# A body of half width for an expert's last rows, one packed table value an expert, and unrolled programs on ScalarE and VectorE

## The chip, the cores and the metric

The kernel runs on one core of a Trainium2 chip. What is compared is the device time of one launch in microseconds: 1143.42 us, the median of three timed runs (1143.06 to 1143.54). The core has TensorE (matmuls), VectorE, ScalarE and GpSimd, and SyncE, which issues most of the DMAs. Each of them runs its own program, and they meet only in semaphores.

## The reference

One transformer layer for 8 sequences of 512 rows and 256 columns: cross-attention with 16 heads over a context of 1024 rows, then a mixture of experts. The feed-forward half is what matters here:

```python
ys = _geglu(xf @ Ws1 + bs1) @ Ws2 + bs2
logits = (xf @ Wr + br) / TAU
top_val, top_idx = jax.lax.top_k(logits, 2)
top_w = jax.nn.softmax(top_val, axis=-1)
...
h = jnp.einsum('nd,edh->enh', xf, We1) + be1[:, None, :]
act = _geglu(h)
yE = jnp.einsum('enh,ehd->end', act, We2) + be2[:, None, :]
yr = jnp.einsum('end,ne->nd', yE, w)
return (ys + yr).reshape(B, T, Dm)
```

There are 4096 rows and 12 experts, and every row goes to two of them, so the experts work on 8192 rows in all. An expert's hidden layer is 2 x 768 wide; `_geglu` multiplies one half of it by the gelu of the other. A kernel need not compute an expert for rows that didn't choose it: this one sorts.

## The kernel before

Attention writes each row, normalised, into a region of `expert_in` in DRAM for each of its two experts, one region an expert. In `feed_forward` VectorE's `tables()` works out how many blocks of `NB` = 256 rows each expert has (`blocks_i`) and the number of its first block (`first_i`), and for each block where in `expert_in` it starts. The shared feed-forward `ys` is done in blocks of the same size; after it the expert stage runs from about 605 us to the end.

*The order of the work.* Nothing is scheduled by a planner: each engine runs the same nest of loops, written by `experts(eng, before, body, piece)` at line 1954. It loops over pairs of experts (`half`, line 1991; the sixth pair is written out behind the loop), so that the buffers of even and odd experts have fixed addresses. At the start of a pair `both` reads four table values into registers. `one` then walks an expert's blocks: on every engine a turn for block `t` is run only if `t < n`, so an expert of three blocks has one empty turn of the four (`FEW`); a copy of the body for blocks from the fifth on lies behind it and is jumped over by experts of at most four. ScalarE and VectorE have one more copy ahead, of two turns (`lead`), in which they also split the next expert's weights into a high and a low half in 16 bits, twelve pieces, one beside each of the six pairs of a block. If an expert has fewer than two blocks, the pieces of the missing ones are done alone.

*A block.* Its rows come from `expert_in` to `ff_xrow` (`load_rows` on SyncE, line 2051; the row's weights and target follow in `ff_rowmeta`). TensorE transposes them (line 2156) during the block before; ScalarE and VectorE make the high half `xh` and the low half `xl`. In `ffn` (line 2160) TensorE then makes the hidden layer in six pairs `j`: 2 halves x 2 tiles x 3 products = 12 matmuls of 128x128 weights on 256 columns. For each pair ScalarE takes the gelu (`ff_gel`, line 2236), VectorE multiplies (`ff_actf`, 2373), ScalarE makes the high half (`ff_acth`, 2231), VectorE the low one (`ff_actl`, 2366). TensorE may be three pairs ahead (three banks). Then it transposes the next block's rows, and the output layer follows: for each pair, for each of the two tiles of 128 rows, 3 matmuls (line 2182). VectorE adds the bias (`ff_ysb`, 2437; one addition for each tile), ScalarE scales by the row's weight (`ff_ysc`, 2282), and GpSimd adds the rows to the output with two indirect DMAs (line 2140). `ff_ysc` is a single buffer: the scaling of a block waits until the DMAs of the block before have landed (`row_done`). So is `ff_rowmeta`: SyncE loads the next one when GpSimd has taken the targets (`t_set`), and issues the rows of the block after that behind it.

*Between experts* GpSimd waits for the split of the expert's weights, sets `ff_taken` and issues the load of the weights of the expert after next (2.3 MB); ScalarE and VectorE copy the expert's biases (`biases_ready`, lines 2270 and 2441); TensorE waits for the split weights (line 2211).

Of the kernel before, what the change touches and what calls it, by code (L numbers as in the profile page):

```python
# [10 lines left out]
P = 128  # L11
# [1801 lines left out]
FEW = 4  # L1813
SH_PAIRS, EX_PAIRS = HS // P, HR // P
# [33 lines left out]
SEEN = 4  # L1848
LISTS = [(0, 0), (0, 1), (1, 0), (1, 1), (1, 2), (1, 3)]
# [4 lines left out]
def feed_forward(nc, io, keep, scratch, shared, expert, early):  # L1854
# [17 lines left out]
    first_i = sb("first_i", [P, E + 1], I32)  # L1872
# [33 lines left out]
    b1a = sb("b1a", [P, EX_PAIRS], FP32)  # L1906
    b1g = sb("b1g", [P, EX_PAIRS], FP32)
# [17 lines left out]
    e_now = sb("e_now", [P, 1], FP32)  # L1925
# [16 lines left out]
    b2_loaded, e_set, g_set, a_set = (semaphore(n) for n in ("b2_loaded", "e_set", "g_set", "a_set"))  # L1942
# [11 lines left out]
    def experts(eng, before, body, piece=None):  # L1954
# [3 lines left out]
        def one(half, u, n, at, last):  # L1958
            e = half * 2 + u
            if before:  # L1960
                before(e, u, last)

            def own(t, beside=None):
                with eng.If(t < n):
                    body(e, u, nc.s_assert_within(at + t, 0, NBLK - 1, skip_runtime_bounds_check_because=
                                               "t < n, and an expert's last block is within all experts' blocks"), beside)

            lead = 0
            if piece and (not last or u == 0):
# [8 lines left out]
            with eng.Fori(lead, FEW) as t:  # L1978
                own(t)
            with eng.If(n > FEW):  # L1980
                with eng.Fori(1, N // NB // FEW) as group:
                    with eng.If(n > group * FEW):
                        with eng.Fori(0, FEW) as t:
                            own(group * FEW + t)

        def both(half, last):
            sizes = [table(eng, blocks_i, half * 2 + u, N // NB) for u in range(2)]
            firsts = [table(eng, first_i, half * 2 + u, NBLK - 1) for u in range(2)]
            for u in range(2):
                one(half, u, sizes[u], firsts[u], last)  # L1990
# [12 lines left out]
    def _(sp):  # L2003
# [60 lines left out]
        experts(sp, None, lambda e, u, n, beside: load_rows(n + 1))  # L2064
        until(expert, "meta_loaded", of(expert, "meta_loaded", table(sp, first_i, E, NBLK), 16))
# [426 lines left out]
```

## Time and profile before

| | |
|---|---|
| median of the timed runs | 1143.42 us |
| the profiled execution | 1138.47 us |
| its span, first to last instruction | 1136.9 us |
| TensorE busy over the span | 994.1 us (87%) |
| VectorE, ScalarE, GpSimd busy | 722.5, 578.4, 369.9 us |
| mean granted clock of TensorE | 0.969 |
| expert stage | 605 us to the end |

Busy time of TensorE counts pipelined matmuls, whose ends are modelled; how long a group takes from start to start is told by the chain of waits better. "Issue" is time in which an engine waited for nothing that the profile shows: it is where its sequencer reads tables, branches, or has no code yet. A row's line is that of the kernel's source, and the lines 1952 to 1991 are those of the loops around a block.

### The profile page before, as it was taken

What the parts mean: (1) busy time and instruction counts of PE and PEld (TensorE: products, weight loads), DVE (VectorE), ACT (ScalarE), POOL (GpSimd) and SP (SyncE); (2) the same over time, 40 slices, a digit from 0 to 9 for tenths busy, and PEclk for the clock granted to TensorE, in tenths of its full rate; (3) what the DMA queues carried; (4) which work ended last, traced back from release to release, by engine and by line L of the source; (5) the groups of instructions that cost most, each with busy time, mean ns of one, the idle gap of its engine ahead of it and who ended that gap; (6) DMA issues with size and microseconds to landing.
All of it is one profiled execution on the core that took longest, in us unless ns stands there. A gap on an engine that the chain in (4) does not pass through costs nothing.

```text
span 1136.9 us, 26307 instructions
## 1 busy us (share of the span) xinstructions
PE 994.1 (87%) x7659; PEld 729.5 (64%) x7660; DVE 722.5 (64%) x1862; ACT 578.4 (51%) x1289; POOL 369.9 (33%) x536
## 2 busy tenths in 40 slices
PE   5678889888998879788998998979998999898995
PEld 3233434444443438676777887869887888787884
DVE  5766777777787645455775765657565666565653
ACT  2135555555555664233534655646454664555652
POOL 5200121435426352073001433334233343333332
PEclk9789999999999999989999999989999999999998
DMA  5524414334532222168434434244233452424232
GB/s 154 140 69 104 99 62 123 96 104 132 126 94 76 99 79 69 40 236 273 149 110 133 103 66 119 42 123 121 44 91 77 116 128 40 123 44 116 48 49 29
DMA packets 105808, 114.98 MB, mean 101 GB/s; under 512 B 20092, under 2 KB 97864, under 8 KB 105552
## 3 DMA queue, kind: packets, MB, share of 16 engines
q1 hardware_dynamic: 85072, 66.08, 21.2%
q0 software_dynamic: 20064, 47.20, 16.8%
q8 instruction: 31, 0.51, 0.2%
q14 instruction: 81, 0.66, 0.2%
q10 hardware_dynamic: 560, 0.53, 0.1%
HBM read 73.64 MB, written 37.25 MB: 98 GB/s over the span
## 4 chain that ended last, share of the span: by engine, by line
PE 38%; issue 8%; DMA 5%; DVE 2%; ACT 1%; POOL 1%; SPq 1%; ACTq 1%; POOLq 0%; DVEq 0%
PE ff_psH L2171 23%; PE ff_psY L2182 14%; DMA ff_xrow<-expert_in 2%; DMA out_dram<-ff_ysc,ff_trow 2%; PE ff_psX L2156 2%; DMA ff_xrow<-xn 1%; DVE ff_actf L2373 1%; DVE ff_actl L2366 1%; DVE ff_ysb L2437 0%; ACTq L1952 0%; DMA out_dram<-ff_x 0%; SPq L1952 0%; ACT ff_ysc L2282 0%; POOL out_dram L2140 0%; ACT ff_wx L2257 0%
## 5 line engine op out<-in xcount | busy, mean ns | idle before, releaser
L2171 PE MATMUL ff_psH<-xh,ff_wx 128*128 128x256 f16 x1872 | 321.1, 276 | 27.3 <-issue 23.0
L2171 PE MATMUL ff_psH<-xl,ff_wx 128*128 128x256 f16 x936 | 258.4, 276 | 0.0
L1122 DVE TENSOR_REDUCE fast_negm<-fast_psS 128x2 f32<-128x512 f32 x256 | 169.2, 686 | 86.6 <-PE fast_psS L513 85.0
L2171 PEld LDWEIGHTS ff_psH<-xh,ff_wx 128*128 128x128 f16 x1872 | 185.4, 99 | 55.9 <-issue 25.8
L884 ACT ACTIVATE fast_PT<-fast_psT 128x512 f32<-128x512 f32 x256 | 145.7, 598 | 71.4 <-PE fast_psT L545 71.1
L2140 POOL DMA_INDIRECT out_dram<-ff_ysc,ff_trow x78 | 123.5, 1583 | 168.2 <-ACT ff_ysc L2282 142.6
L2373 DVE SCALAR_TENSOR_TENSOR ff_actf<-ff_psH,ff_b1a,ff_gel 128x256 f32<-128x256 f32 x234 | 112.5, 481 | 89.4 <-ACT ff_gel L2236 89.3
L2182 PE MATMUL ff_psY<-ff_wx,ff_acth 128*128 128x256 f16 x936 | 155.4, 273 | 0.0
L2236 ACT ACTIVATE ff_gel<-ff_psH,ff_b1g 128x256 f32<-128x256 f32 x234 | 109.5, 468 | 60.4 <-PE ff_psH L2171 49.8
L2231 ACT ACTIVATE ff_acth<-ff_actf 128x256 f16<-128x256 f32 x282 | 115.6, 410 | 29.1 <-DVE ff_actf L2373 27.0
L2182 PE MATMUL ff_psY<-ff_wx,ff_actl 128*128 128x256 f16 x468 | 127.6, 273 | 0.0
L513 PE MATMUL fast_psS<-fast_Kz,fast_Qs 128*128 128x512 f16 x256 | 98.3, 396 | 29.6 <-DVE fast_negm L1122 21.7
L2366 DVE TENSOR_TENSOR ff_actl<-ff_actf,ff_acth 128x256 f16<-128x256 f32 x282 | 117.6, 417 | 4.0 <-ACT ff_acth L2231 1.9
L545 PE MATMUL fast_psT<-fast_Qs,fast_Kz 128*128 128x512 f16 x256 | 96.7, 383 | 12.6 <-ACT fast_PT L884 12.2
L2171 PEld LDWEIGHTS ff_psH<-xl,ff_wx 128*128 128x128 f16 x936 | 92.8, 99 | 11.4
L2182 PEld LDWEIGHTS ff_psY<-ff_wx,ff_acth 128*128 128x128 f16 x936 | 91.6, 98 | 10.1
L2282 ACT ACTIVATE ff_ysc<-ff_ysb,ff_wrow 128x256 f32<-128x256 f32 x78 | 35.4, 500 | 113.8 <-DVE ff_ysb L2437 113.8
L2395 DVE TENSOR_TENSOR ff_wx<-ff_st,ff_wx x144 | 79.9, 555 | 15.7 <-ACT ff_wx L2257 11.5
L1456 POOL TENSOR_SCALAR fast_rstd<-fast_mv 128x4 f32<-128x4 f32 x16 | 3.6, 227 | 221.1 <-DVE fast_mv L1074 196.1
L2257 ACT ACTIVATE ff_wx<-ff_st x144 | 73.8, 512 | 1.6 <-issue 1.3
L545 PEld LDWEIGHTS fast_psT<-fast_Qs,fast_Kz 128*128 128x128 f16 x256 | 24.8, 99 | 75.0 <-ACT fast_PT L884 41.7
L561 PE MATMUL fast_psV<-fast_PT,fast_V 128*32 128x512 f32 x512 | 69.1, 612 | 3.1 <-ACT fast_PT L884 1.7
(260 smaller groups left out, 1621.3 us busy)
## 6 DMA issues: line engine op xcount, KB each, us to landing
ff_st<-in_L_ffn_We_dram POOLq DMA_DIRECT2D x12, 1536.0 KB, 7.3
ff_xrow<-expert_in SPq DMA_DIRECT2D x40, 256.0 KB
ff_st<-in_L_ffn_We_dram POOLq DMA_DIRECT2D x12, 768.0 KB, 8.9
fast_Qs<-qstk SPq DMA_DIRECT2D x48, 128.0 KB
fast_xbuf<-in_x_dram SPq DMA_DIRECT2D x8, 512.0 KB, 4.9
fast_words<-in_mask_BxSxS_bk_dram SPq DMA_DIRECT2D x8, 512.0 KB, 3.8
fast_xres<-in_x_dram SPq DMA_DIRECT2D x8, 512.0 KB, 4.0
out_dram<-fast_x1s SPq DMA_DIRECT2D x8, 512.0 KB, 5.0
```

What stands on the lines that cost most here:

```text
L513: mm = nc.tensor.matmul(out[:], qs(b)[:, p, t * P:(t + 1) * P], kz(b, c)[:, p, :, :], start=True, stop=not general)
L545: mm = nc.tensor.matmul(out[:], kz(b, kb // 2)[:, h // 2, h % 2, (kb % 2) * P:(kb % 2 + 1) * P], qs(b)[:, h // 2, :], start=True, stop=not ...
L884: nc.scalar.activation(PT[:, n % NPT, :], psT[n % 2][:], ACT.Exp).then_inc(sem["exp_done"], 1)
L1122: nc.vector.tensor_reduce(negm[:, two(b), t, 2 * p:2 * p + 2], src, AX.X, ALU.max, negate=True).then_inc(sem["max_done"], 1)
L2140: pool.indirect_dma_start(out=out_rows, out_offset=bass.IndirectOffsetOnAxis(ap=trow[:, j:j + 1], axis=0), in_=ysc[:, j, :], in_offset=Non ...
L2171: mm = nc.tensor.matmul(psH[j % stage.banks][:, half * NB:(half + 1) * NB], a[:, dt, lo:lo + P], x[:, dt, :], start=(dt == 0 and i == 0), ...
L2182: mm = nc.tensor.matmul(psY[i][:, 0:D], a[:, j, i * P:(i + 1) * P], x[:, j, :], start=(j == 0 and s == 0), stop=(j == n - 1 and s == 2))
L2231: nc.scalar.activation(acth[:, j, :], actf[:, j % 2, :], ACT.Copy).then_inc(stage.sem["acth"], 1)
L2236: nc.scalar.activation(gel[:, j % 2, :], psH[j % stage.banks][:, NB:2 * NB], ACT.Gelu, bias=gate_bias[:, j:j + 1]).then_inc(stage.sem["gel ...
L2366: nc.vector.tensor_tensor(actl[:, j, :], actf[:, j % 2, :], acth[:, j, :], ALU.subtract)\
L2373: nc.vector.scalar_tensor_tensor(actf[:, j % 2, :], psH[j % stage.banks][:, 0:NB], bias[:, j:j + 1], gel[:, j % 2, :], ALU.add, ALU.mult). ...
L2395: nc.vector.tensor_tensor(wx[u][1][:, cols], st[u][:, cols], wx[u][0][:, cols], ALU.subtract).then_inc(w_low, 1)
```

## The change

What was a block of 256 rows always becomes 256 rows as long as an expert has as many, and its rest, if it is 1 to 128 rows, goes through a body of half width: 128 columns in each hidden matmul, one tile of output rows instead of two, and 128 elements in the four operations of ScalarE and VectorE on a pair. A rest of 129 to 256 rows takes the full body as before. Loading, transposing, scaling and adding to the output stay at 256 rows; the unused half of `ff_ysb` is set to zero once. The number of units of 128 rows and the first block of an expert are packed in one table value (`place_i`), which is taken apart in registers, so that an engine reads one value for an expert instead of two.

TensorE, GpSimd and SyncE keep the loop over pairs of experts; GpSimd and SyncE have no half body. TensorE's single loop of four turns becomes two of two turns, with a test around the second, the copy for the fifth block on is inside that test, and the half body stands behind it. ScalarE and VectorE are written out for the twelve experts, each reading its one value at its start; their copies of the biases go, as the addresses are now fixed.

```diff
-    def experts(eng, before, body, piece=None):
+    def place_of(eng, e):
+        value = nc.values_load(place_i[0:1, bass.ds(e, 1)], engines=[eng.engine], min_val=0, max_val=NBLK * PLACE + PLACE - 1,
+                               skip_runtime_bounds_check_because="built on chip from counts whose sum is two rows a token")
+        return value & (PLACE - 1), value >> PLACE.bit_length() - 1
+
+    def experts(eng, before, body, piece=None, halves=True, unrolled=False):
 
         eng.wait_ge(table_ready, 1)
 
-        def one(half, u, n, at, last):
-            e = half * 2 + u
+        def one(e, u, units, at, last):
             if before:
                 before(e, u, last)
+            n = (units >> 1) if halves else (units + 1) >> 1
+
+            def block_at(t):
+                return nc.s_assert_within(at + t, 0, NBLK - 1, skip_runtime_bounds_check_because=
+                                          "t < n, and an expert's last block is within all experts' blocks")
 
             def own(t, beside=None):
                 with eng.If(t < n):
-                    body(e, u, nc.s_assert_within(at + t, 0, NBLK - 1, skip_runtime_bounds_check_because=
-                                               "t < n, and an expert's last block is within all experts' blocks"), beside)
+                    body(e, u, block_at(t), beside, NB)
 
             lead = 0
-            if piece and (not last or u == 0):
+            if piece and not last:
                 lead = PIECES // EX_PAIRS
                 with eng.Fori(0, lead) as t:
                     def beside(j):
-                        piece(e + 1, half + (1 + u), 1 - u, at, t * EX_PAIRS + j, j == 0)
+                        piece(e + 1, (e + 1) // 2 + 1, 1 - u, at, t * EX_PAIRS + j, j == 0)
                     own(t, beside)
                     with eng.If(t >= n):
                         for j in range(EX_PAIRS):
                             beside(j)
-            with eng.Fori(lead, FEW) as t:
-                own(t)
-            with eng.If(n > FEW):
-                with eng.Fori(1, N // NB // FEW) as group:
-                    with eng.If(n > group * FEW):
-                        with eng.Fori(0, FEW) as t:
-                            own(group * FEW + t)
+            if lead < FEW // 2:
+                with eng.Fori(lead, FEW // 2) as t:
+                    own(t)
+            with eng.If(n > FEW // 2):
+                with eng.Fori(FEW // 2, FEW) as t:
+                    own(t)
+                with eng.If(n > FEW):
+                    with eng.Fori(1, N // NB // FEW) as group:
+                        with eng.If(n > group * FEW):
+                            with eng.Fori(0, FEW) as t:
+                                own(group * FEW + t)
+            if halves:
+                with eng.If((units & 1) > 0):
+                    body(e, u, block_at(n), None, UN)
+
+        if unrolled:
+            for e in range(E):
+                one(e, e % 2, *place_of(eng, e), e == E - 1)
+            return
 
         def both(half, last):
-            sizes = [table(eng, blocks_i, half * 2 + u, N // NB) for u in range(2)]
-            firsts = [table(eng, first_i, half * 2 + u, NBLK - 1) for u in range(2)]
+            places = [place_of(eng, half * 2 + u) for u in range(2)]
             for u in range(2):
-                one(half, u, sizes[u], firsts[u], last)
+                one(half * 2 + u, u, *places[u], last)
         with eng.Fori(0, E // 2 - 1) as half:
             both(half, False)
         both(E // 2 - 1, True)
...
-        def ffn(stage, m, wa, wb, more):
+        def ffn(stage, m, wa, wb, more, rows=NB):
...
-                            mm = nc.tensor.matmul(psH[j % stage.banks][:, half * NB:(half + 1) * NB], a[:, dt, lo:lo + P],
-                                                  x[:, dt, :], start=(dt == 0 and i == 0), stop=(dt == DT - 1 and i == 2))
+                            mm = nc.tensor.matmul(psH[j % stage.banks][:, half * NB:half * NB + rows], a[:, dt, lo:lo + P],
+                                                  x[:, dt, 0:rows], start=(dt == 0 and i == 0), stop=(dt == DT - 1 and i == 2))
...
-                for i in range(NBT):
+                for i in range(rows // P):
...
-                nc.scalar.activation(gel[:, j % 2, :], psH[j % stage.banks][:, NB:2 * NB], ACT.Gelu,
+                nc.scalar.activation(gel[:, j % 2, 0:rows], psH[j % stage.banks][:, NB:NB + rows], ACT.Gelu,
...
-        def biases_ready(e, u, last):
-            nc.scalar.activation(b1g[:], b1T[:, bass.ds((e * 2 + 1) * EX_PAIRS, EX_PAIRS)], ACT.Copy).then_inc(g_set, 1)
-            act.wait_ge(g_set, e + 1)
-            if not isinstance(e, int):
-                act.sem_inc(alone, 1)
...
-        experts(act, biases_ready, expert_rows, high_piece)
+        experts(act, None, expert_rows, high_piece, unrolled=True)
...
+            then(nc.vector.scalar_tensor_tensor(first[:], first[:], float(PLACE), units[:], ALU.mult, ALU.add))
+            nc.vector.tensor_copy(place_i[:], first[:])
...
-        experts(dve, biases_ready, expert_block, low_piece)
+        experts(dve, None, expert_block, low_piece, unrolled=True)
```

TensorE, the end of an expert's first copy of the body. Before, `L1978` ends the loop of four turns and `L1980` jumps over the copy for blocks from the fifth on, one copy of 245 instructions (a weight load, which has no row of its own here, counted with each matmul):

```order
L2182 MATMUL ff_psY<-ff_wx,ff_acth 128x256 x2
L2182 MATMUL ff_psY<-ff_wx,ff_actl 128x256
L1964 UNCONDITIONAL_BRANCH
L1978 REGISTER_ALU
L1978 COMPARE_AND_BRANCH
L1980 COMPARE_AND_BRANCH
L1981 UNCONDITIONAL_BRANCH
```

Now `L1989` ends a loop of two turns and `L1991` jumps over two copies, 491 instructions:

```order
L2204 MATMUL ff_psY<-ff_wx,ff_acth 128x256 x2
L2204 MATMUL ff_psY<-ff_wx,ff_actl 128x256
L1975 UNCONDITIONAL_BRANCH
L1989 REGISTER_ALU
L1989 COMPARE_AND_BRANCH
L1991 REGISTER_ALU x2
L1991 COMPARE_AND_BRANCH
L1992 UNCONDITIONAL_BRANCH
L1975 COMPARE_AND_BRANCH
```

Its target is the test for the half body, whose hidden matmuls have 128 columns:

```order
L2000 REGISTER_ALU
L2000 COMPARE_AND_BRANCH
L79 ISA x2
L2193 MATMUL ff_psH<-xh,ff_wx 128x128
L2193 MATMUL ff_psH<-xl,ff_wx 128x128
L2193 MATMUL ff_psH<-xh,ff_wx 128x128 x2
```

With two such parts the loop over pairs, from the table loads to its branch back, grows from 996 instructions to 1880.

ScalarE, from the end of one expert to the first gelu of the next. Before, at the end of a pair (`L1991` branches back to the first load of the loop; these loads are those of the last pair, which look the same):

```order
L1991 REGISTER_ALU
L1991 COMPARE_AND_BRANCH
L1952 TENSOR_LOAD ff_blocks_i
L1952 ISA x2
L1952 TENSOR_LOAD ff_blocks_i
L1952 ISA x2
L1952 TENSOR_LOAD ff_first_i
L1952 ISA x2
L1952 TENSOR_LOAD ff_first_i
L1952 ISA x2
L2271 ACTIVATE ff_b1g<-ff_b1T 128x6
L1971 UNCONDITIONAL_BRANCH
```

Now, between two experts that are written out one behind the other:

```order
L2298 ACTIVATE ff_ysc<-ff_ysb,ff_wrow 128x256 x2
L2000 UNCONDITIONAL_BRANCH
L1957 TENSOR_LOAD ff_place_i
L1981 UNCONDITIONAL_BRANCH
L1975 REGISTER_ALU x2
L1975 COMPARE_AND_BRANCH
L79 ISA
L79 REGISTER_ALU
L2258 ACTIVATE ff_gel<-ff_psH,ff_b1T 128x256
```

Three loads of four, the copy of the biases and the branch back are gone, and the stored program is longer: an expert has about 160 instructions on ScalarE and 190 on VectorE, times twelve.

## Rows read from the trace of the kernel before

**Rows 1.** Busy time by stretch: expert stage, and start of expert 4.

```profile
core 0: us, PE busy (x) PEld busy (x) DVE busy (x) ACT busy (x) POOL busy (x), PEclk, DMA share, GB/s
608.62:1124.30 515.68, 487.74 (x4368) 430.45 (x4368) 314.50 (x817) 293.62 (x726) 181.04 (x264) 0.98 0.38 87
757.00:762.00 5.00, 3.28 (x16) 2.35 (x17) 0.33 (x2) 0.00 (x0) 2.52 (x2) 0.50 0.63 104
```

**Rows 2.** Chain of waits: start us, us, what; one full block.

```profile
661.16 7.86 PE ff_psH L2171 x72
669.02 0.44 PE ff_psX L2156 x4
669.45 3.93 PE ff_psY L2182 x36
```

**Rows 3.** Page, part 5: the output DMAs, two a block.

```profile
L2140 POOL DMA_INDIRECT out_dram<-ff_ysc,ff_trow x78 | 123.5, 1583 | 168.2 <-ACT ff_ysc L2282 142.6
```

**Rows 4.** VectorE's timeline: start us, us; additions of a block's result.

```profile
673.54 0.76 DVE L2437 TENSOR_TENSOR ff_ysb<-ff_psY,ff_b 128x256 f32<-128x256 f32 x2 [1.83 <-PE ff_psY L2182]
685.76 0.76 DVE L2437 TENSOR_TENSOR ff_ysb<-ff_psY,ff_b 128x256 f32<-128x256 f32 x2 [1.83 <-PE ff_psY L2182]
...
703.63 0.76 DVE L2437 TENSOR_TENSOR ff_ysb<-ff_psY,ff_b 128x256 f32<-128x256 f32 x2 [0.65 <-PE ff_psY L2182]
...
753.71 0.76 DVE L2437 TENSOR_TENSOR ff_ysb<-ff_psY,ff_b 128x256 f32<-128x256 f32 x2 [0.63 <-PE ff_psY L2182]
...
773.11 0.76 DVE L2437 TENSOR_TENSOR ff_ysb<-ff_psY,ff_b 128x256 f32<-128x256 f32 x2 [0.92 <-PE ff_psY L2182]
...
917.17 0.84 DVE L2437 TENSOR_TENSOR ff_ysb<-ff_psY,ff_b 128x256 f32<-128x256 f32 x2 [1.84 <-PE ff_psY L2182]
...
929.58 0.76 DVE L2437 TENSOR_TENSOR ff_ysb<-ff_psY,ff_b 128x256 f32<-128x256 f32 x2 [0.66 <-PE ff_psY L2182]
...
942.82 0.76 DVE L2437 TENSOR_TENSOR ff_ysb<-ff_psY,ff_b 128x256 f32<-128x256 f32 x2 [0.60 <-PE ff_psY L2182]
...
967.29 0.76 DVE L2437 TENSOR_TENSOR ff_ysb<-ff_psY,ff_b 128x256 f32<-128x256 f32 x2 [1.83 <-PE ff_psY L2182]
...
985.63 0.76 DVE L2437 TENSOR_TENSOR ff_ysb<-ff_psY,ff_b 128x256 f32<-128x256 f32 x2 [0.65 <-PE ff_psY L2182]
```

**Rows 5.** Chain of waits at the branches back before experts 2 and 4.

```profile
687.26 3.02 issue
...
690.37 0.28 ACTq L1952
...
691.01 0.27 ACTq L1952
...
753.55 5.17 issue
758.72 9.86 PE ff_psH L2171 x72
```

**Rows 6.** Table loads: ns min/median/max, first and last start.

```profile
L1952 ACTq TENSOR_LOAD <-ff_blocks_i x12: 272/283/381, 603.6 to 1050.9; - x12
L1952 PEldq TENSOR_LOAD <-ff_blocks_i x12: 296/307/323, 604.5 to 1048.3; - x12
```

**Rows 7.** TensorE's branches: over unexecuted code, and back (ns min/median/max).

```profile
L2002 PEldq COMPARE_BRANCH  x1: 3485/3485/3485, 481.1 to 481.1; - x1
...
L1991 PEldq COMPARE_BRANCH  x5: 76/208/219, 684.3 to 1047.5; - x5
```

**Rows 8.** DMA queues, 700 to 1040 us: packets, MB, share; q8 has none.

```profile
q0 software_dynamic: 11040, 25.43, 31.5%
q1 hardware_dynamic: 14144, 7.03, 8.6%
q14 instruction: 33, 0.27, 0.3%
```

**Rows 9.** TensorE's timeline: matmuls of one column, each with its load.

```profile
594.99 1.94 PE L2206 MATMUL ff_psB<-ones,ff_wx 128*128 128x1 f16 x72
```

**Rows 10.** Groups by line, expert stage: busy us, mean ns; idle before.

```profile
L2171 PEld LDWEIGHTS ff_psH<-xh,ff_wx 128*128 128x128 f16 x1872 | 185.4, 99 | 55.9 <-issue 25.8 <-DVE ff_actf L2373 6.5
...
L2373 DVE SCALAR_TENSOR_TENSOR ff_actf<-ff_psH,ff_b1a,ff_gel 128x256 f32<-128x256 f32 x234 | 112.5, 481 | 89.4 <-ACT ff_gel L2236 89.3
L2236 ACT ACTIVATE ff_gel<-ff_psH,ff_b1g 128x256 f32<-128x256 f32 x234 | 109.5, 468 | 60.4 <-PE ff_psH L2171 49.8 <-ACT ff_b1g L2271 4.1
L2366 DVE TENSOR_TENSOR ff_actl<-ff_actf,ff_acth 128x256 f16<-128x256 f32 x238 | 99.2, 417 | 3.0 <-ACT ff_acth L2231 1.5
L2231 ACT ACTIVATE ff_acth<-ff_actf 128x256 f16<-128x256 f32 x238 | 97.5, 410 | 21.2 <-DVE ff_actf L2373 19.2
...
L2395 DVE TENSOR_TENSOR ff_wx<-ff_st,ff_wx x132 | 73.2, 554 | 13.9 <-ACT ff_wx L2257 11.5 <-issue 2.3
L2257 ACT ACTIVATE ff_wx<-ff_st x132 | 67.6, 512 | 1.6 <-issue 1.3
...
L2222 ACT ACTIVATE xh<-ff_psX 128x512 f16<-128x512 f32 x40 | 23.1, 578 | 0.0
```

**Rows 11.** VectorE's timeline: the last low half ahead of expert 4.

```profile
752.06 0.42 DVE L2366 TENSOR_TENSOR ff_actl<-ff_actf,ff_acth 128x256 f16<-128x256 f32 x1
```

**Rows 12.** Landing of a scatter in the chain; TensorE's waits for rows.

```profile
639.50 3.74 DMA out_dram<-ff_ysc,ff_trow
...
PE ff_psX L2156 <- DMA ff_xrow<-expert_in: 4.0, 5, 1.3
```

More of the change, by code:

```diff
@@ L1813 @@
 FEW = 4
+UN = P
 SH_PAIRS, EX_PAIRS = HS // P, HR // P
@@ L1848 @@
 SEEN = 4
+PLACE = 64
 LISTS = [(0, 0), (0, 1), (1, 0), (1, 1), (1, 2), (1, 3)]
@@ L2063, in _ @@
         store_out(NSH - 1)
-        experts(sp, None, lambda e, u, n, beside: load_rows(n + 1))
-        until(expert, "meta_loaded", of(expert, "meta_loaded", table(sp, first_i, E, NBLK), 16))
+        experts(sp, None, lambda e, u, n, beside, rows: load_rows(n + 1), halves=False)
+        until(expert, "meta_loaded", of(expert, "meta_loaded", table(sp, total_i, 0, NBLK), 16))
         until(shared, "saved", of(shared, "saved", NSH))
@@ L2125, in start_expert, with add_rows @@
                 load_weights(e + 2, u)
-        def add_rows(e, u, n, beside):
+        def add_rows(e, u, n, beside, rows):
             expert.until(pool, "meta_loaded", of(expert, "meta_loaded", n, 16), alone=True)
@@ L2144, in add_rows @@
             pool.sem_inc(expert.sem["row_done"], 1)
-        experts(pool, start_expert, add_rows)
+        experts(pool, start_expert, add_rows, halves=False)
     @block.tensor
@@ L2214, in weights_ready @@
                 pe.sem_inc(alone, 1)
-        experts(pe, weights_ready, lambda e, u, n, beside: ffn(expert, n, w1[u], w2[u], (expert, n + 1)))
+        experts(pe, weights_ready, lambda e, u, n, beside, rows: ffn(expert, n, w1[u], w2[u], (expert, n + 1), rows))
     @block.scalar
@@ L2222, in row_high, with ffn @@
             nc.scalar.activation(xh[:].rearrange("p t n -> p (t n)"), psX[:], ACT.Copy).then_inc(stage.sem["xh"], 1)
-        def ffn(stage, m, gate_bias, more, beside=None):
+        def ffn(stage, m, gate_bias, more, beside=None, rows=NB):
             n = stage.pairs
@@ L2230, in high @@
                     stage.until(act, "y_mm", of(stage, "y_mm", m))
-                nc.scalar.activation(acth[:, j, :], actf[:, j % 2, :], ACT.Copy).then_inc(stage.sem["acth"], 1)
+                nc.scalar.activation(acth[:, j, 0:rows], actf[:, j % 2, 0:rows], ACT.Copy).then_inc(stage.sem["acth"], 1)
             for j in range(n):
@@ L2304, in tables @@
             then(nc.vector.tensor_scalar(counts_i[:], counts[:], float(NB - 1), None, ALU.add))
+            nc.vector.tensor_scalar(units[:], counts[:], float(UN - 1), None, ALU.add)
             then(nc.vector.tensor_scalar(blocks_i[:], counts_i[:], NB.bit_length() - 1, None, ALU.logical_shift_right))
+            then(nc.vector.tensor_copy(units_i[:], units[:]))
+            then(nc.vector.tensor_scalar(units_i[:], units_i[:], UN.bit_length() - 1, None, ALU.logical_shift_right))
+            nc.vector.tensor_copy(units[:], units_i[:])
             dve.wait_ge(cleared, 1)
@@ L2357, in row_low, with ffn @@
                                     ALU.subtract).then_inc(stage.sem["xl"], 1)
-        def ffn(stage, m, bias, more, result, beside=None):
+        def ffn(stage, m, bias, more, result, beside=None, rows=NB):
             n = stage.pairs
```

50 lines of the change are left out of this document (22 added, 28 removed).

## The prediction

> **What bounds the kernel now.** I read the page first, for TensorE's share, then the stretches around the expert stage, then the chain of waits of that stage, then VectorE's timeline at the experts' borders, last the code that the borders run and the instruction DMAs.
>
> From 608.6 to 1124.3 us the kernel does nothing but expert blocks, and TensorE is busy for 487.7 of 515.7 us [rows 1]. In the chain a full block of 256 rows is TensorE alone: 7.86 us for the 72 matmuls of the hidden layer, 0.44 us for the next block's transposes, 3.93 us for the 36 of the output layer, together 12.23 us [rows 2]. The output DMAs are 78, two a block, so 39 blocks ran [rows 3], and 39 x 12.23 = 477.0 us; the other 38.7 us lie at the borders of experts. The distance between two result additions on VectorE shows where: 12.22 us inside an expert, 17.87 (685.76 to 703.63), 19.40 and 18.34 us where the loop over pairs of experts jumps back, and 12.41 plus 13.24 us where expert 7 follows 6 [rows 4]. The four jumps back (before experts 2, 4, 6, 8) lose 5.6, 7.2, 6.2 and 6.1 us over 12.23, 25.1 in all, though after each of them every engine reads its tables again. On ScalarE 3.02 us of nothing stand right behind the loop's branch, and only then come the four table loads [rows 5]; a load takes 0.28 us on ScalarE and 0.31 on TensorE [rows 6], on ScalarE about 0.6 from one to the next [rows 5], so on TensorE, whose register work is no shorter, some 0.75. TensorE's own branch back costs 0.21 us and never more than 0.22, but its branch over unexecuted code at 481 us took 3.49 us [rows 7]. Between 700 and 1040 us instruction queue q8, which moved 31 packets of 16 KB over the span (page, part 3) and which I take for TensorE's, moved nothing, though the loop ran round several times [rows 8]. So TensorE's loop (996 instructions, a weight load counted for each matmul) stays in its memory, and those of ScalarE and VectorE (293 and some 340) do not.
>
> **The change, part by part.** From the reference's inputs the experts get 371, 831, 614, 487, 1296, 738, 520, 802, 720, 621, 676, 516 rows. In blocks of 256 that is 39, as the trace has it; in units of 128 it is 70: 31 full bodies and 8 half ones (experts 0, 1, 2, 4, 6, 7, 9, 11).
>
> *Half bodies.* 72 hidden matmuls keep their weight loads and have 128 columns for 256; 36 output matmuls become 18 of unchanged shape; the transposes stay. No 128-column matmul in 16 bits is in the trace. From below: half of 0.109 us is 0.055; from above, if the weight load set the pace, 0.109. 72 loads with one column each took 1.94 us [rows 9], 0.025 us apart, so loads don't set it: 72 x 0.056 = 4.0, + 0.44 + 18 x 0.109 = 2.0, is 6.4 us. ScalarE and VectorE must keep up with 0.67 us a pair: at 256 columns an activation and a copy take 0.47 + 0.41, the two VectorE operations 0.48 + 0.42 [rows 10]. Copies of 256, 384 and 512 columns take 0.41, 0.51, 0.58, so 128 columns save about 0.1 each and a pair needs some 0.65 to 0.7. That leaves the last pair's chain of four small operations sticking out; I take 6.8 us, between 6.4 and 7.8. Eight times 12.23 - 6.8 = 5.4 is **-43.4 us** (-35 to -47).
>
> The Trainium skill speaks against small matmuls: "TensorE: Matmul & The Clock Gate" (Wait — 56ns, not 53.3ns?) gives about 62 ns of sequencer time for each matmul when hardware decode is off. The 0.025 us spacing [rows 9] shows that this doesn't hold here; by it a half body would take some 0.4 us more.
>
> *Expert 0* has one full block. ScalarE and VectorE do the second six pieces of weight splitting with no matmul beside them, before the half body: 6 x 0.51 and 6 x 0.55 us [rows 10] that were hidden. With TensorE's first skip (below) **+4.8**.
>
> *The loop back.* ScalarE and VectorE run straight on: their 3 us gap, three of four loads and two small copies go, so they are ready about 3 us after a block's end and TensorE decides. Its sequencer is 1.1 us ahead of its matmuls: the last low half ends at 752.48, the matmuls at 753.55, and the next ones start at 758.72 [rows 5, 11]. These 6.3 us hold four loads (3.0) and, after an expert of two blocks, two empty loop turns of two 0.21 us branches with their register work each (1.45). After the change two loads remain and the empty iterations are skipped: 3.3 us. I take it as lost: 3.3 us more (3.49 less 0.21 [rows 7]), and the idle time costs 2 us at 1.2 GHz: after the wait of 5.17 us the granted clock was 0.50 [rows 1] and the same 72 matmuls took 9.86 us [rows 5]. Behind a half body the sequencer is only 0.3 us ahead. The four borders then lose 8.6, 7.5, 6.5 and 8.6 = 31.2 for 25.1: **+6.1** (between -14 and +12).
>
> The rule behind this is in "Runtime: NRT & Kernel Launch" (Instruction fetch mechanics): 128 KiB for TensorE, filled in blocks of 16 KiB, and a taken branch out of the window waits for a fetch. By it 1880 instructions of 64 bytes, 117.5 KiB, with a block fetched ahead don't fit; the trace agrees in size with its 3.49 us branch, and has no run of this size.
>
> *Skips.* An expert of one or two full blocks now jumps over two unused copies, 491 instructions or 1.9 pieces; before it was one, 0.95 piece, and cost nothing. The new jump lands beyond the next piece. I count it where the code is reached for the first time: expert 0 (above) and 11, **+3.6** (3.5 + 1.2 of branches - 1.1 ahead). In the loop's later passes the piece may still be there.
>
> *Borders without a jump back.* Before experts 1, 3, 5, 7 TensorE now starts 1 us late (short lead behind a half body). The chain scatter, its landing (3.74 us), target rows, metadata, next rows had 20.1 us from a block's end and already made TensorE wait up to 1.3 us [rows 3, 12]. A half body brings the scatter 1.5 us closer to the one before it. Together about 2.6 us a border where 1.9 were lost: **+3.6**, and **+0.4** before expert 10, which has no branch back but also the short lead.
>
> *The rest.* First start two loads less, -1.3; at the end the last scatter waits for its predecessor, +1. The table's five added VectorE operations and GpSimd's memset lie beside shared blocks, where TensorE is busy; uncovered they would be 1.5 us.
>
> Sum: -43.4 + 4.8 + 6.1 + 3.6 + 3.6 + 0.4 - 0.3 = -25.2. The profiled execution took 1138.5 us, so 1113.3; the median of the timed runs is 4.95 above it, so **1118 us**.
>
> **The rivals.** *A, TensorE's code stays.* For it: q8's silence; against: the loop nearly doubles. The four borders lose 10 to 12 us for 25.1 (-13 for +6.1), expert 11 nothing: -47.9, **1095 us**.
>
> *B, the forecast*: lost at each jump back, kept otherwise.
>
> *C, all its code is fetched anew in each pass*, as the other engines' is now (33 pieces on their queue between 700 and 1040 us [rows 8]). Then the skip also costs at experts 2, 6 and 9 (3.6 each, less 2.8 that hide the row waits), expert 3 stops for its skips twice more and expert 5 once (3.3 each): +18, **1136 us**, within noise of no gain from below.
>
> *D, the weight load sets the pace of narrow matmuls.* Page part 5 has a load at 99 ns and matmuls 109 ns apart [rows 10]. At 0.109 each, a half body's hidden layer stays at 7.86 and loses 72 x 0.054 = 3.9 us, eight times 31: **1149 us**, slower. It turns the result from 0.1 us a matmul on. Against it stands the 0.025 us spacing.
>
> *E, the change doesn't do what it says*: other row counts, fewer halves. 39 blocks fit the counts; 0.01.
>
> **How the numbers follow.** B 0.40, A 0.22, C 0.27, D 0.05, the rest 0.06. B's own range, by the half body and the borders, is 1108 to 1128. The 8-in-10 range takes in A and most of C: 1092 to 1142. A measurement tells 0.2%, 2.3 us, from no change. A and B are faster, C is in two thirds of its spread, D is slower: faster 0.80, same 0.09, slower 0.11.
>
> **What would show it.** Half bodies: result additions 6.4 to 7.8 us apart, 128-column matmuls 0.056 us apart; at 0.109 it is D. ScalarE's and VectorE's "issue" waits at borders under 3 us. TensorE: branch rows of the loop back at about 3.5 us and q8 active between experts 2 and 9 for B and C, silent for A; 3.5 us at experts 2, 3, 6, 9 for C. Wrong I would be if half bodies took over 8 us, or if TensorE waited at a border for rows for more than 3 us.

## The result and the profile after

The changed kernel took 1148.58 us (median of 8 runs, 1145.5 to 1153.11), the kernel before 1143.24 us on the same chip. The ratio is 1.006, with a 95% interval of 1.0038 to 1.0082: about 6 us slower. Forecast were 1118 us. Of the kernels below, dead_code alone had runs more than 1.5% slower than its fastest; these two of its four are left out of its ratio.

First the page of the profiled execution (1145.5 us, span 1143.6): busy time by engine, the instruction queue that I had taken for TensorE's, and the costliest group with its idle time (31 packets, and 23.0 us for want of instructions, in the kernel before).

```profile
PE 967.9 (85%) x7515; PEld 704.6 (62%) x7516; DVE 709.5 (62%) x1834; ACT 568.7 (50%) x1276; POOL 366.2 (32%) x537
...
q8 instruction: 73, 1.20, 0.4%
...
L2193 PE MATMUL ff_psH<-xh,ff_wx 128*128 128x256 f16 (+1 forms) x1872 | 302.6, 273 | 62.2 <-issue 60.1
```

The windows of the expert stage, of the wait before expert 4 and of the block behind it. They answer to [rows 1]: stretch, length, busy time by engine, granted clock, DMA share, GB/s.

```profile
608.74:1130.90 522.16, 455.90 (x4224) 404.20 (x4224) 300.63 (x786) 284.06 (x715) 175.81 (x260) 0.94 0.38 87
760.60:770.60 10.00, 10.00 (x74) 8.25 (x75) 5.25 (x13) 5.65 (x14) 2.65 (x7) 0.79 0.58 222
755.00:761.00 6.00, 0.40 (x3) 0.29 (x4) 0.00 (x0) 0.00 (x0) 1.55 (x1) 0.50 0.56 93
```

The stage takes 522.2 us for 515.7, though TensorE is busy for 31.8 us less: it is idle for 66.3 us where it was for 27.9, and its granted clock fell from 0.98 to 0.94.

The chain of waits (start us, us, what) shows a half body, and what stands before expert 4, which answers to the 5.17 us of [rows 5].

```profile
746.89 3.93 PE ff_psY L2204 x36
750.82 9.78 issue
760.60 10.02 PE ff_psH L2193 x72
...
912.45 4.19 PE ff_psH L2193 x72
...
917.08 1.98 PE ff_psY L2204 x18
```

The body itself is what was forecast: with 0.44 us of transposes between the two rows it takes about 6.6 us, and 6.4 where nothing disturbs it; its 128-column matmuls start 0.056 us apart. Behind the full block before it, though, TensorE waits 2.66 us for want of instructions. The wait before expert 4 has nearly doubled. VectorE's additions say the same, against [rows 4]:

```profile
750.85 0.76 DVE L2458 TENSOR_TENSOR ff_ysb<-ff_psY,ff_b 128x256 f32<-128x256 f32 x2 [0.64 <-PE ff_psY L2204]
775.02 0.75 DVE L2458 TENSOR_TENSOR ff_ysb<-ff_psY,ff_b 128x256 f32<-128x256 f32 x2 [1.16 <-PE ff_psY L2204]
...
909.83 0.76 DVE L2458 TENSOR_TENSOR ff_ysb<-ff_psY,ff_b 128x256 f32<-128x256 f32 x2 [1.31 <-PE ff_psY L2204]
919.09 0.42 DVE L2458 TENSOR_TENSOR ff_ysb<-ff_psY,ff_b 128x256 f32<-128x256 f32 x1
```

24.17 us over the border before expert 4 (19.40 before the change); 9.3 us for expert 6's half body with the skip ahead of it. All eight half bodies are 8.6 to 14.0 us from the addition before, though the prediction had 6.4 to 7.8 and named over 8 us as a sign of being wrong. Over the four borders with a jump back the distances are 20.05, 24.17, 23.92 and 19.88 us: 39.1 us over 12.23, for 25.1.

TensorE's branches, ns min/median/max, first and last start (in [rows 7] the branch back never took over 219). L1991 jumps over two copies of the body (the one for the third and fourth block and the one for blocks from the fifth on), L2000 over the half body, L2012 is the branch back.

```profile
L1991 PEldq COMPARE_BRANCH  x12: 67/198/4496, 620.7 to 1120.5; - x12
L2000 PEldq COMPARE_BRANCH  x12: 68/77/3388, 625.4 to 1124.1; - x12
L2012 PEldq COMPARE_BRANCH  x5: 67/3604/4593, 681.7 to 1055.4; - x5
```

From 600 us on, 13 of these branches take 2.1 to 4.6 us, 45.6 us in all: four at the branch back, four at L2000 (behind experts 3, 5, 8 and 10, which have no half body), five at L1991 (experts 0, 2, 6, 9 and 11). Three of them, at expert 0, behind expert 10 and at expert 11, are at code that is reached for the first time: experts 10 and 11 are the sixth pair, written out behind the loop. Behind expert 3 two come in a row, 3.14 us at 750.58 and 4.59 us at 753.88; these are the 9.78 us of the chain. Between 700 and 1040 us, where q8 was silent [rows 8], it moves 31 packets:

```profile
q8 instruction: 31, 0.51, 0.6%
```

### The profile page after: what moved, and what is told of

Its sections match the earlier page's. It is cut to its first block, busy times and chain, and to the rows that moved or that the text cites. A ratio compares the mean times of both kernels' runs of the same rounds, so it can differ in the third digit from the quotient of the medians.

```text
span 1143.6 us, 25763 instructions
## 1 busy us (share of the span) xinstructions
PE 967.9 (85%) x7515; PEld 704.6 (62%) x7516; DVE 709.5 (62%) x1834; ACT 568.7 (50%) x1276; POOL 366.2 (32%) x537
## 4 chain that ended last, share of the span: by engine, by line
PE 39%; issue 10%; DMA 4%; DVE 2%; SPq 1%; ACT 1%; POOL 1%; POOLq 0%; DVEq 0%; ACTq 0%
PE ff_psH L2193 25%; PE ff_psY L2204 13%; PE ff_psX L2178 2%; DMA ff_xrow<-expert_in 2%; DMA out_dram<-ff_ysc,ff_trow 1%; DMA ff_xrow<-xn 1%; DVE ff_actl L2387 1%; DVE ff_actf L2394 0%; POOL out_dram L2162 0%; SPq L1954 0%; ACT ff_ysc L2298 0%; DMA out_dram<-ff_x 0%; ACT ff_gel L2258 0%; PE ff_psB L2228 0%; DVE ff_ysb L2458 0%
## 5 line engine op out<-in xcount | busy, mean ns | idle before, releaser
L2193 PE MATMUL ff_psH<-xh,ff_wx 128*128 128x256 f16 (+1 forms) x1872 | 302.6, 273 | 62.2 <-issue 60.1
L2193 PE MATMUL ff_psH<-xl,ff_wx 128*128 128x256 f16 (+1 forms) x936 | 249.2, 273 | 0.0
L2394 DVE SCALAR_TENSOR_TENSOR ff_actf<-ff_psH,ff_b1T,ff_gel 128x256 f32<-128x256 f32 (+1 forms) x234 | 106.2, 454 | 153.1 <-ACT ff_gel L2258 151.8
L2258 ACT ACTIVATE ff_gel<-ff_psH,ff_b1T 128x256 f32<-128x256 f32 (+1 forms) x234 | 105.8, 452 | 122.3 <-PE ff_psH L2193 109.2
L2204 PE MATMUL ff_psY<-ff_wx,ff_acth 128*128 128x256 f16 x840 | 140.5, 274 | 0.0
L2253 ACT ACTIVATE ff_acth<-ff_actf 128x256 f16<-128x256 f32 (+1 forms) x282 | 110.1, 390 | 22.6 <-DVE ff_actf L2394 21.2
L2204 PE MATMUL ff_psY<-ff_wx,ff_actl 128*128 128x256 f16 x420 | 114.8, 273 | 0.0
L2387 DVE TENSOR_TENSOR ff_actl<-ff_actf,ff_acth 128x256 f16<-128x256 f32 (+1 forms) x282 | 111.0, 393 | 4.1 <-ACT ff_acth L2253 3.0
L2193 PEld LDWEIGHTS ff_psH<-xl,ff_wx 128*128 128x128 f16 x936 | 96.5, 103 | 10.0
L2204 PEld LDWEIGHTS ff_psY<-ff_wx,ff_acth 128*128 128x128 f16 x840 | 82.5, 98 | 9.5
L545 PEld LDWEIGHTS fast_psT<-fast_Qs,fast_Kz 128*128 128x128 f16 x256 | 25.1, 100 | 76.9 <-ACT fast_PT L884 40.0
```

Source lines behind the costliest of these rows:

```text
L545: mm = nc.tensor.matmul(out[:], kz(b, kb // 2)[:, h // 2, h % 2, (kb % 2) * P:(kb % 2 + 1) * P], qs(b)[:, h // 2, :], start=True, stop=not ...
L2193: mm = nc.tensor.matmul(psH[j % stage.banks][:, half * NB:half * NB + rows], a[:, dt, lo:lo + P], x[:, dt, 0:rows], start=(dt == 0 and i = ...
L2204: mm = nc.tensor.matmul(psY[i][:, 0:D], a[:, j, i * P:(i + 1) * P], x[:, j, :], start=(j == 0 and s == 0), stop=(j == n - 1 and s == 2))
L2253: nc.scalar.activation(acth[:, j, 0:rows], actf[:, j % 2, 0:rows], ACT.Copy).then_inc(stage.sem["acth"], 1)
L2258: nc.scalar.activation(gel[:, j % 2, 0:rows], psH[j % stage.banks][:, NB:NB + rows], ACT.Gelu, bias=gate_bias[:, j:j + 1]).then_inc(stage. ...
L2387: nc.vector.tensor_tensor(actl[:, j, 0:rows], actf[:, j % 2, 0:rows], acth[:, j, 0:rows], ALU.subtract)\
```

## The experiments

**Theory 1:** TensorE's pair loop, grown from 996 to 1880 instructions (1878 in the texts and pads below), no longer stays in the engine's memory, and its code is fetched anew in each pass. **Theory 2:** the long jump over two unused copies costs it, whatever the loop's size. **Theory 3:** something else of the change is at fault (unrolled programs of ScalarE and VectorE, half bodies). The first four kernels ran on one chip (kernel before: 1142.57 us), the seven others on a second one (1179.24 and 1180.39 us). There the expert stage begins some 34 us later and takes the same time: the kernel short_loop, traced on both, has its first hidden matmul of an expert at 609.4 and 643.3 us, and from there to its last matmul 487.0 and 484.7 us. So between the chips only ratios are compared.

**short_loop.** The changed kernel, but TensorE has one loop of four turns for an expert's full bodies: 1396 instructions.

```
-            if lead < FEW // 2:
-                with eng.Fori(lead, FEW // 2) as t: own(t)
-            with eng.If(n > FEW // 2):
-                with eng.Fori(FEW // 2, FEW) as t: own(t)
+            with eng.Fori(0, FEW) as t: own(t)      # TensorE alone
```

> The changed kernel with one edit on TensorE alone: one loop of four turns over an expert's blocks, as before, instead of two of two turns, so one full copy less for each expert and a loop over pairs of 1396 instructions instead of 1878. Theory 1 (TensorE's loop no longer stays in its memory, and its branches wait for code): all branches of 2 to 4.6 us vanish, q8 moves nothing in the middle of the expert stage, and most of their 47 us come back: 1095 to 1108 us. Theory 2 (the half bodies and the earlier work of the other engines bring waits of their own, for rows or for GpSimd, and the branches only hide them): 1135 to 1150 us.

Measured: 1112.33 us, ratio 0.973 (0.9711 to 0.9749). Of 13 long branches two are left, both where code is reached for the first time; q8 and the branch back:

```profile
q8 instruction: 34, 0.56, 0.2%
...
L2020 PEldq COMPARE_BRANCH  x5: 76/207/212, 680.9 to 1018.8; - x5
```

This one loop turns 1.006 into 0.973, some 38 us, more than the whole error of the forecast, though unrolled programs and half bodies are still in it. Theory 3 falls as the cause of the loss. Theory 1's 1095 to 1108 us is missed by 4 us all the same: with its code in place the kernel has other waits, below.

**dead_code.** The kernel before with 219 matmuls for each expert behind conditions that are never true; TensorE's loop has 1878 instructions.

```
+                if unused:
+                    with eng.If(n > N // NB - 1): unused(121)
+            if unused:
+                with eng.If(n > N // NB - 1): unused(98)
```

> The kernel before, with matmuls that are never executed placed where the changed kernel has its extra copies on TensorE (121 after the copy for blocks from the fifth on, 98 more behind it, for each expert; the loop over pairs is 1878 instructions long, as in the changed kernel). Nothing else changes, what is executed is the same. Theory 1: long branches at the same places as in the changed kernel, some 10 of 3 to 4.6 us, and 1170 to 1190 us. Theory 2: code that isn't executed costs two tests an expert, 1143 to 1148 us.

Measured: 1198.64 and 1214.71 us, ratio 1.0558 (1.0475 to 1.0641); the trace is of an execution of 1227.0 us. From 600 us on 24 of its branches take 1.9 us or more, 87.1 us together: twelve at the added skip of 98 matmuls, one for each expert, nine at the skip over the copy and the other 121, three at the branch back. q8 moves 72 packets. Code that is never executed costs 6%, more than the 1170 to 1190 us expected, and half of the long branches stand at a jump that the changed kernel doesn't have. So this run doesn't tell size from jumps.

**unrolled_only** and **halves_only.** Both have short_loop's TensorE loop. The first has no half bodies (the rest of an expert takes a full one), the second keeps ScalarE's and VectorE's rolled loop with its three small copies an expert. Both have the packed table value; no run has it alone.

```
-            n = (units >> 1) if halves else (units + 1) >> 1
+            n = (units + 1) >> 1                    # unrolled_only; no body for UN rows
```

```
-        experts(act, None, expert_rows, high_piece, unrolled=True)
+        experts(act, biases_ready, expert_rows, high_piece)     # halves_only; VectorE likewise
```

> Short TensorE loop, packed table value, ScalarE and VectorE unrolled, but no half bodies. Theory 1: their gaps of 3 us behind the branch back and three loads of four go, TensorE decides at the borders, the four borders with a branch back lose 8 to 13 us instead of 25: 1128 to 1135 us. Theory 2 (the longer programs of ScalarE and VectorE wait for code themselves, or GpSimd's chain takes over): 1140 us or more.

> Short TensorE loop, packed table value, half bodies, but ScalarE and VectorE in the loop over pairs as before. Theory 1: eight half bodies of 6.4 us instead of 12.23 save 47 us, less 3 at expert 0 and 1 to 1.5 at each border behind a half body; the branch back of ScalarE and VectorE stays: 1103 to 1113 us. Theory 2: above 1125 us.

Measured: 1126.01 us, ratio 0.986 (0.9834 to 0.9886), and 1114.18 us, ratio 0.9758 (0.9736 to 0.978). Both lie just outside what was expected, 2 us below and 1 us above. Each part gains without the other, 17 and 28 us (the packed value counted in both), but together 30, not 45. Beside unrolling, half bodies give 14 us, though they take 46.6 us of work away; beside half bodies, unrolling gives 1.9 us, less than the runs of each kernel spread. TensorE's waits in the expert stage (in total, times, longest us), of unrolled_only and then of short_loop, say where the rest goes:

```profile
PE ff_psH L2198 <- issue: 17.6, 12, 3.9
```

```profile
PE ff_psH L2201 <- issue: 29.0, 14, 3.9
PE ff_psX L2186 <- DMA ff_xrow<-expert_in: 10.8, 6, 2.3
PE ff_psH L2201 <- DVE ff_actf L2402: 2.2, 2, 1.7
PE ff_psH L2201 <- DVE xl L2385: 2.0, 5, 1.2
```

26.4 us of waits come back. 10.8 of them are waits for rows, which unrolled_only doesn't have, and 11.4 are for want of instructions. These stand inside the experts: of the 29.0 us, 14.1 are seven waits of 1.1 to 3.0 us right ahead of half bodies, where in unrolled_only one block follows the other without a wait. What is left, 14.9 us at the starts of experts, is no more than in unrolled_only. So in short_loop expert 6's half body of 6.4 us, which nothing disturbs, has its result 7.87 us behind that of the full block ahead of it:

```profile
886.43 0.76 DVE L2466 TENSOR_TENSOR ff_ysb<-ff_psY,ff_b 128x256 f32<-128x256 f32 x2 [1.31 <-PE ff_psY L2212]
894.30 0.42 DVE L2466 TENSOR_TENSOR ff_ysb<-ff_psY,ff_b 128x256 f32<-128x256 f32 x1
```

**pad_1642, pad_1760, pad_1878.** short_loop with 122, 181 or 240 matmuls that are never executed, between the two experts of a pair on TensorE: one taken jump a pass, and the loop's size.

```
+            if unused and u == 0 and not last:
+                with eng.If(n > N // NB - 1): unused()   # 122, 181 or 240 matmuls
```

> The kernel short_loop (TensorE's block loop as one loop of four turns, pair loop of 1396 instructions, 1112 us) with 122 matmuls behind a never-true condition between the two experts of a pair: the loop has 1642 instructions and nothing more is executed than one taken branch a pass. Theory 1 (what counts is whether TensorE's whole pair loop stays in its memory): if the limit lies above 1642, no long branches, q8 as in short_loop (34 packets), 1111 to 1116 us; if it lies below, branches of about 3.5 us in each of five passes, 1130 to 1150 us. Theory 2 (it was the jump over two unused block copies, however long the loop is): one skip of 246 instructions is as short as that of the kernel before, so 1111 to 1116 us.

> The same with 240 matmuls behind the condition: a pair loop of 1878 instructions, as long as that of the changed kernel, with one skip of 482 instructions a pass. Theory 1: code lost in each pass, branches of 3 to 5 us at the jump back, at the skip and inside the experts, q8 above 60 packets, 1135 to 1160 us. Theory 2: the one skip costs 3.5 us in each of five passes, 17 us, and the jump back nothing: 1125 to 1133 us. If the loop stays: 1111 to 1116 us.

> As pad_1642 and pad_1878, with 181 matmuls that are never executed: a pair loop of 1760 instructions. At 1642 the loop stayed (ratio 0.975 to the kernel before), at 1878 it was lost in every pass (1.030). Theory a (a sharp limit: all stays or all is lost in each pass): 0.973 to 0.977, or 1.02 to 1.035, and q8 at 35 or about 70 packets. Theory b (the loss grows with the size over the limit): in between, 0.98 to 1.01, q8 at 40 to 60 packets.

Measured, with the branch back (ns min/median/max) of each, in this order:

| loop | ratio to before | branches over 1.3 us after 600 us | q8 packets |
|---|---|---|---|
| 1642 | 0.9747 (0.9705 to 0.9789) | 2, 4.8 us | 35 |
| 1760 | 1.0126 (1.0097 to 1.0156) | 12, 41.3 us | 71 |
| 1878 | 1.0298 (1.0252 to 1.0344) | 13, 46.3 us | 71 |

```profile
L2023 PEldq COMPARE_BRANCH  x5: 76/208/215, 719.9 to 1058.8; - x5
```

```profile
L2023 PEldq COMPARE_BRANCH  x5: 76/3624/5462, 721.4 to 1101.4; - x5
```

```profile
L2023 PEldq COMPARE_BRANCH  x5: 79/3591/5368, 727.0 to 1123.6; - x5
```

The same code with 246 dead instructions costs nothing that can be told from short_loop (0.973), with 364 it costs 4% over it and with 482 nearly 6%. The limit lies between 1642 and 1760 instructions, and above it the branch back costs 3.6 us at the median. It is sharp in packets and long branches, as theory a had it; in time the loss still grows. The ratio at 1760, 1.0126, is in neither theory's range, and 1878 is dearer than the 1135 to 1160 us expected. At 1760 the chain has 12.10 us of waiting in one piece, and the hidden layer behind it takes 10.75 us for 7.86:

```profile
791.15 12.10 issue
803.25 10.75 PE ff_psH L2204 x72
```

At 1878 there is one long branch more and 20 us more of time. TensorE's waits for want of instructions (in total, times, longest us) grow by 20.0 us, first 1760, then 1878:

```profile
PE ff_psH L2204 <- issue: 71.1, 20, 12.1
```

```profile
PE ff_psH L2204 <- issue: 91.1, 22, 11.5
```

16 us of it stand behind the skip over the dead code, at the first matmuls of experts 1, 3, 5, 7 and 9: 1.8 to 7.4 us at 1760, 4.5 to 10.5 us at 1878. So code that is away costs more than the branch rows show. The changed kernel, which has as many long branches but no such skip between its experts, waits 60.1 us. Why the target of the longer skip comes later, these runs don't tell.

**split_only.** The kernel before with its TensorE loop split as in the change; 1478 instructions, and a jump over two copies (491 instructions) where an expert has two blocks.

```
+                with eng.Fori(0, FEW // 2) as t: own(t)
+                with eng.If(n > FEW // 2):
+                    with eng.Fori(FEW // 2, FEW) as t: own(t)
```

> The kernel before with only TensorE's block loop split in two loops of two turns (pair loop 1478 instructions; experts 0 and 3, with two blocks, jump over two unused copies, 491 instructions; no half bodies, no unrolling). Theory 1: 1478 instructions stay resident; no long branches from expert 2 on, 1139 to 1146 us, against 1143 us of the kernel before; one first-time skip at expert 0 may cost 3.5 us. Theory 2 (the long skip does it): 3.5 to 5 us at experts 0 and 3 each and again at the next jump back, 1150 to 1158 us.

Measured: ratio 1.0031 (1.0003 to 1.0058), q8 34 packets, two long branches, both at code reached for the first time (3.42 us at expert 0, 3.05 at the end). Expert 3's jump over two copies and the branch back behind it cost nothing: over the four borders with a branch back the additions lose 25.2 us against 12.23 a block, where it was 25.1. Theory 2 falls: a jump of 491 instructions is free in a loop that stays, so it isn't the 364 of pad_1760 that cost.

**rows_ahead, and rows_again beside short_again.** short_loop's chain at a border shows why rows come late. Start us, us, what:

```profile
818.78 0.28 ACT ff_ysc L2306
...
822.43 4.24 DMA out_dram<-ff_ysc,ff_trow
...
829.13 0.20 POOL ff_taken L2151
...
830.47 1.34 issue
...
832.77 0.21 POOL ff_filled L2159
...
833.64 0.19 POOL ff_trow L2165
...
836.11 4.84 DMA ff_xrow<-expert_in
841.00 0.66 PE ff_psX L2186 x4
```

The row queue asks for a block's rows behind the metadata of the block ahead of it, these wait for GpSimd's target rows, and GpSimd first waits for the scatter to land, walks its loop's branches and starts the next weights. From the scatter's landing to the target rows it takes 7 us. The edit asks for rows first:

```
-        load_rows(n + 1):  rows of n + 1, then metadata of n + 1
+        load_rows(n + 2)   # as soon as the transposes of n + 1 are done
+        load_meta(n + 1)
```

> short_loop with another order on the queue that loads rows: the rows of block n+2 are asked for as soon as those of n+1 are transposed, ahead of the metadata of block n+1, which waits for the target rows and so for the scatter before. In short_loop TensorE waits six times for rows, 1.4 to 2.6 us (10.8 us between 700 and 1040 us). Theory (the chain scatter, its landing, target rows, metadata, rows took back a part of what the half bodies give): these waits go, 1098 to 1104 us. Rival (the same chain only moves: metadata then come late and VectorE and GpSimd hold the results back): 1108 to 1114 us.

> The kernel short_loop once more, on the same chip as rows_again, so that the two can be compared directly: 0.972 to 0.975 of the kernel before.

> The kernel rows_ahead once more, beside short_again. TensorE's five to seven waits for rows (7 to 11 us) were gone from its trace. If they lay on the path that sets the end, it stands 6 to 10 us below short_again; if the time only moved to the borders' other waits, less than 3 us.

Measured: rows_ahead 0.9692 (0.9653 to 0.9732), which on the first chip would be 1107 us, between what theory and rival expected; then on one chip short_again 1146.90 us, ratio 0.9725 (0.9698 to 0.9752), and rows_again 1141.36 us, ratio 0.9666 (0.9631 to 0.97). TensorE's waits from 640 to 1135 us, in short_again and then in rows_again:

```profile
PE ff_psH L2201 <- issue: 28.1, 14, 3.5
PE ff_psX L2186 <- DMA ff_xrow<-expert_in: 7.9, 6, 2.6
PE ff_psH L2201 <- DVE ff_actf L2402: 3.0, 2, 2.5
PE ff_psH L2201 <- DVE xl L2385: 2.1, 3, 1.2
```

```profile
PE ff_psH L2218 <- issue: 29.2, 18, 4.3
PE ff_psH L2218 <- DVE ff_actf L2419: 3.7, 3, 2.4
PE ff_psH L2218 <- DVE xl L2402: 2.7, 4, 1.3
PE ff_psY L2229 <- DVE ff_actl L2412: 2.2, 7, 0.4
```

The 7.9 us of waits for rows are gone, and the medians are 5.5 us apart. The intervals just overlap, so the gain is probable rather than certain, and it is a little less than the 6 to 10 us expected: waits on VectorE grew from 5.1 to 8.6 us, which may be the part that is missing. This is the best version that ran: 3.3% below the kernel before.

## Why the prediction was wrong, step by step

**Half bodies** (-43.4): right for the body itself, with a little in hand. 8 x (12.23 - 6.4) is -46.6, and rival D, the weight load as the pace, is refuted by the 0.056 us spacing. But what TensorE waits ahead of a half body and in it was put at nothing, apart from experts 0 and 11, and it is the largest miss of the sum, below.

**The rest of the stage.** Before, it lost 38.7 us beside its bodies. The forecast's other terms make that 57.2 (+4.8, +6.1, +3.6, +3.6, +0.4). In the trace it is 522.2 - 31 x 12.23 - 8 x 6.4 = 91.9. These 34.7 us, less 3.2 from the half bodies, are all but 0.7 us of the error of the profiled execution (1145.5 for 1113.3). VectorE's additions say where they lie. Each distance is counted over 12.23 us for a full block and 6.4 for a half one; the forecast's 8 x 0.4 us stand with the half bodies.

| place | before | forecast | measured | short_loop |
|---|---|---|---|---|
| half bodies | | 11.6 | 33.4 | 22.3 |
| first blocks of experts 2, 4, 6, 8 | 25.1 | 31.2 | 39.1 | 11.1 |
| first blocks of experts 9 and 11 | 0.2 | 0.2 | 9.1 | 6.8 |
| full blocks of experts 1, 3, 5, 7 | 7.5 | 11.1 | 9.1 | 9.7 |
| other full blocks | 4.0 | 4.4 | 1.2 | 6.7 |

**The loop back** (+6.1): the mechanism was right, code lost at the branch back, and the size too small: +14.0. Before experts 2 and 8 it was 7.8 and 7.7 us for 8.6. I had counted one fetch a border; before experts 4 and 6, which lose 11.9 and 11.7 us for 7.5 and 6.5, there are two in a row, 3.1 and 4.5 us, and the clock is down longer: at 0.50 in the wait, at 0.79 over the 10 us behind it. The first of the two is a skip, of the next step. The 3.49 us that I took for the price of a fetch were those of line 2002, where each engine's part of this half of the kernel begins; no row showed that they were a jump over unexecuted code, but the size was right for single long branches.

**Skips** (+3.6, and expert 0's share): this is the first step that failed. It said "I count it where the code is reached for the first time ... In the loop's later passes the piece may still be there." It was not. Long branches stand at experts 2, 6 and 9 and, over the half body, behind 3, 5 and 8, 18.0 us in six rows; none of them was in the sum. A seventh, 3.4 us behind expert 10, wasn't either, but its code is reached for the first time. That is rival C's list, with one less at expert 3 and 8 and 10 added. C was still priced at 1136 for 1148.6: it had no dearer second miss, and no stall inside a body. The changed kernel has three of these, all in half bodies (experts 1, 7 and 9; 1.9, 1.9 and 2.5 us) behind their sixth matmul, with no long branch at that point, and short_loop has none there. This one is expert 7's; a packet of q8 starts at 961.0 us:

```profile
961.36 1.94 issue
```

So what happened was C's mechanism, to which I gave 0.27 against 0.40 for B. Once I took the loop as too large, nothing in the trace spoke for part of it staying. The pads decide it: from the first branch back to the end of expert 9 no branch takes over 1.3 us at 1642 instructions, and eleven do at 1760.

**What a half body waits for with the code in place** (put at nothing): the second step that failed. The forecast charged 22.7 us for lost code, the distance from A to B; taking it away by short_loop gave 36. That is 13.5 us of the 30.6 by which the median was off. The other 17 are A's own error, 1095 us for short_loop's 1112, which has its code in place, though also the empty turns that A had counted out. Of the half bodies' 22.3 us there, A had 8.0. How much of it is branches and how much the chain of the last pair, no run separates.

**Unrolled ScalarE and VectorE:** right in kind. Their 3 us behind the branch are gone, the longest wait for want of instructions on either at a border is 0.4 us. What this is worth, the runs tell less well: unrolled_only gains 17 us, but with the packed table value, and taking the unrolling out of short_loop (halves_only) costs 1.9 us, within the spread of the runs. The sum had put it inside the loop back, where short_loop loses 11.1 us and halves_only 13.9.

**Borders for rows** (+3.6): right in kind. One wait of 3.4 us went over the 3 us that I had named as a limit, but the three make 5.3 us, against 4.0 in [rows 12]. With the code in place the chain shows more, 10.8 us in short_loop, and cuts what half bodies give. Rival A (1095 us), which let the code stay, had the same +3.6 for it.

## What to carry to other kernels

Count an engine's instructions in the innermost loop that must stay, weight loads and unexecuted branches included, before and after an edit; where a loop outgrows the engine's memory, price all its jumps in every pass, not the first one alone. When a shorter body goes between blocks that followed each other without a wait, price the branches that lead to it as well. Splitting a loop for finer control can cost more than the work that it saves, and one shorter loop may give both. When an engine on the path gets half the work, look for the chain that was just hidden: here scatter, target rows, metadata, rows. And measure a part both with and without its neighbour: unrolling looked like 17 us in one pair of runs and like 2 in the other.

## What the runs showed of the hardware

- TensorE's loop stays at 1642 instructions and is fetched anew at 1760, in a program where nothing else changed but the length of a skip, which split_only shows to be free at 491 instructions. The Trainium skill, "Runtime: NRT & Kernel Launch" (Instruction fetch mechanics), gives 128 KiB or 2048 instructions, refilled in order in blocks of 16 KiB. The measured limit lies below that. An estimate from the Trainium skill's figures: 1642 and 1760 instructions are 6.4 and 6.9 blocks of 256, and either can touch eight, with a ninth fetched ahead; so the block size doesn't tell them apart, and why the limit lies between them stays open. That section of the Trainium skill gives no time for a fetch, so the 3.49 us of the prediction agree with it only in that a branch can wait. The Trainium skill also calls the crossing of a block mostly hidden; the 1.94 us inside a body, with a packet of q8 beside it, look like one that isn't.
- Where the code was lost, a branch back by itself took 3.4 to 3.6 us, and one right behind another long branch 4.5 to 5.6 us (nine times in four kernels; once, in dead_code, 0.2 us). A skip right behind a long one took no more than others, 3.0 to 3.7 us, so it isn't the second wait as such that is dearer.
- 128-column matmuls with a weight load each run 0.056 us apart, in proportion to 256 columns at 0.109.
- Two chips gave 1143 and 1180 us for the same kernel, at a granted clock of 0.966 and about 0.952. Short_loop's traces put the difference ahead of the expert stage, and its ratio was the same on both (0.973 and 0.9725).
